# A two-layer mixture-of-experts tower on one core: reciprocal roots by Newton steps on VectorE, one gelu per unit, and four passes written out

## The chip, the cores and the metric

The kernel runs on one core of a Trainium2 chip. The time is the device time of one execution, in microseconds (us). It was taken three times; the median is what is to be forecast. One more execution was recorded by the hardware profiler; all rows below are from it. The engines are TensorE (PE, with its weight loads as PEld), VectorE (DVE), ScalarE (ACT), GpSimd (POOL) and SyncE (SP, which issues the transfers).

## What is computed

Sixteen sequences of 256 tokens go through an embedding and four blocks, each with a residual. The first RWKV block with its channel mix comes first and is not touched. Then come a dense mixture of eight experts, a second RWKV block, and an attention block with a mixture of four experts:

```python
# dense mixture: every expert computes every token (layer 0)
h = gelu(einsum('td,edh->eth', xf, W1) + b1, approximate=False)      # 8 experts, 1024 hidden
out = einsum('etd,te->td', einsum('ehd...', h, W2) + b2, weights)    # weights: softmax over the top 2
# attention (layer 1): 16 heads of 16, q and k normalised per head
_rms = lambda x, w: x * rsqrt(mean(x * x, -1) + EPS) * w
q, k, v = _rms(heads(wq), qn_w), _rms(heads(wk), kn_w), heads(wv)
attn = softmax(causal(q @ k.T * 16 ** -0.5));  x = x + (attn @ v) @ wo.T
# mixture of layer 1: gelu experts o0, o2, o3, and o1 = silu(xf @ e1_w1.T) * (xf @ e1_w2.T) @ e1_down.T
```

The change concerns `gelu`, the `rsqrt` of q and k in `_rms`, and the code of the loop over tokens.

## The kernel before

Matrix products are done in bfloat16 in three parts (high by high, low by high, high by low), so each activation is needed as a rounded half `hi` and a remainder `lo`. Phase A (the embedding and the first RWKV block) fills the first 458 us. After it, `phase_bc` goes over eight tiles of 512 tokens in ten passes. In pass i three streams are woven together: the dense mixture of tile i, the *front* of tile i-1 (RWKV, then attention, two sequences or four 128-token groups `s` to a tile), and the second-layer experts of tile i-2. Pass 0 has the dense mixture alone, pass 1 adds the front, passes 2 to 6 have all three (order `ORDER_BC`), pass 7 has dense units and front (`ORDER_B`), pass 8 front and experts of two tiles (`ORDER_CC`), and pass 9 only experts.

**Order.** Every engine runs the same list of steps. `ORDER_F` is a string of front steps with numbers between them; `plan.braid` puts dense and expert units in where the numbers leave room. `go` walks the list and each engine does its own part of each step. So an engine's queue is fixed, and what stands behind a waiting instruction waits as well.

**Units.** A dense unit `U` (lines 2247 on PE) or a gelu expert unit `I` (line 2000) computes a 128 x 512 product into one of two PSUM banks, `ub[n % 2]` (in rows: `c_up`). ACT reads the bank twice with Gelu: line 1569 writes `g` in float32 (`c_g`), line 1570 writes `hi` in bfloat16 (`c_hi`). POOL then computes `lo` = `g` - `hi` (line 1408). PE may overwrite the bank two units later, when `hi` is written (`bank_free`). The gated expert `G` uses tanh (1560), two DVE operations (1922, 1926) and a copy of `g` to `hi` (1562). The down products (2264, with bias product 2261; experts 2320) add up in PSUM, and DVE takes them into the residual with a weight per token (line 1937, `h`).

**The keys.** For each 128-token group `s`, PE computes q and k (step `Q`), ACT squares and copies them (`Qx`, lines 1485 to 1490), and DVE sums the squares per head (`squares`, 1764), makes the mean (1767) and its reciprocal (1769), and the remainder of v (1771). After two groups, step `X` has ACT take the square root of the reciprocals, 128 x 64 (1497, `c_qrs`). Step `K` on DVE multiplies q and k by it and by the gains and splits them (1779, 1784, 1791 to 1794, 1796, 1798); step `T` has PE transpose them (2090). This happens for groups 0 and 1 (called b0 here) and again for groups 2 and 3 (b1) of each tile. The second group's K and T come after the first's.

**Table loads.** ACT holds one set of functions at a time. Gelu, exp and the square root are in different sets, and a change shows as `ACT_TABLE_LOAD` at the line that needs it.

**The loop.** Passes 0 to 2 and 7 to 9 are written out. Passes 3 to 6 are one hardware loop (`Fori(3, TILES - 1)`) on every engine and on SP's stream of weights.

## Time and profile before

| | before |
|---|---|
| time, median of 3 (range) | 3157.91 us (3155.34 to 3163.25) |
| the profiled execution: time / span | 3164.51 us / 3162.7 us |
| PE busy | 2791.1 us, 88% |
| DVE busy | 1643.0 us, 52% |
| ACT busy | 1819.6 us, 58% |
| POOL busy | 1428.1 us, 45% |

A span is what the trace covers; the time has about 1.8 us around it. Busy time is that in which an engine executes something other than register, branch, semaphore and transfer-issuing instructions. "L" with a number is the line of the kernel.

### The profile page before, as it was taken

To read this page: it belongs to the slowest core of one execution; us is meant where nothing else is said; L and a number is where in the kernel's file an instruction comes from. 1 tells how busy PE (TensorE), PEld (TensorE's weight loads), DVE (VectorE), ACT (ScalarE), POOL (GpSimd) and SP (SyncE) were. 2 spreads that over 40 slices of the span, in tenths; PEclk is the share of its full clock that TensorE was granted. 3 is DMA by queue.
4 is the path that set the end of the run, shared out by engine and by line. 5 is a ranking of instruction groups with operands and counts; after the bars stand their busy time and mean duration, and the time that the engine had idled before them with its cause. 6 is when DMAs were issued, how large, how long until landed. Compare 5 with 4: busy or idle time off the path is not lost. (4 is left out here: it accounts for less than half of the span.)

```text
span 3162.7 us, 58694 instructions
## 1 busy us (share of the span) xinstructions
PE 2791.1 (88%) x22208; PEld 1862.8 (59%) x22208; DVE 1643.0 (52%) x3100; ACT 1819.6 (58%) x2899; POOL 1428.1 (45%) x1358
## 2 busy tenths in 40 slices
PE   3899958998999989998989898989898998987878
PEld 1555535665665666566656675667565765653555
DVE  5776735436446444644365436634563465446452
ACT  3666635555765666565565565565556655654634
POOL 5666523443454435443544454444444443453334
PEclk8999979999999999999999999999999999999999
DMA  1000028621121212121212122212222121210002
GB/s 62 21 27 13 20 74 309 239 102 66 54 92 68 78 68 93 67 82 61 96 68 82 65 81 73 89 64 74 80 82 73 66 74 61 73 41 22 24 23 76
DMA packets 59719, 235.92 MB, mean 75 GB/s; under 512 B 6560, under 2 KB 25024, under 8 KB 40640
## 3 DMA queue, kind: packets, MB, share of 16 engines
q1 hardware_dynamic: 57920, 228.13, 20.6%
q0 software_dynamic: 1536, 4.20, 0.5%
q8 instruction: 176, 2.88, 0.4%
q14 instruction: 87, 0.71, 0.1%
HBM read 200.57 MB, written 31.72 MB: 73 GB/s over the span
## 5 line engine op out<-in xcount | busy, mean ns | idle before, releaser
L1408 POOL TENSOR_TENSOR c_lo<-c_g,c_hi 128x512 bf16<-128x512 f32 x720 | 887.6, 1240 | 1347.0 <-ACT c_hi L1570 1222.3
L2247 PE MATMUL c_up<-c_xT,c_ring 128*128 128x512 bf16 x3072 | 750.8, 384 | 69.3 <-ACT c_hi L1570 56.0
L2264 PE MATMUL c_down<-c_ring,c_hi 128*128 128x256 bf16 x4096 | 715.4, 275 | 0.0
L1569 ACT ACTIVATE c_g<-c_up,b 128x512 f32<-128x512 f32 x512 | 352.9, 689 | 491.1 <-PE c_up L2247 487.1
L2264 PE MATMUL c_down<-c_ring,c_lo 128*128 128x256 bf16 x2048 | 563.3, 275 | 0.0
L2247 PEld LDWEIGHTS c_up<-c_xT,c_ring 128*128 128x128 bf16 x3072 | 295.7, 99 | 367.4 <-ACT c_hi L1570 67.5
L2264 PEld LDWEIGHTS c_down<-c_ring,c_hi 128*128 128x128 bf16 x4096 | 398.3, 99 | 106.0 <-issue 2.2
L1570 ACT ACTIVATE c_hi<-c_up,b 128x512 bf16<-128x512 f32 x512 | 350.9, 685 | 0.0
L1836 DVE CAST c_room<-c_room 128x384 bf16<-128x384 f32 x256 | 128.2, 530 | 403.7 <-PE c_front L2159 307.8
L1569 ACT ACTIVATE c_g<-c_up 128x512 f32<-128x512 f32 x176 | 105.5, 600 | 295.1 <-PE c_up L2000 289.0
L2264 PEld LDWEIGHTS c_down<-c_ring,c_lo 128*128 128x128 bf16 x2048 | 202.1, 99 | 25.0
L1386 POOL TENSOR_TENSOR c_room<-c_room 128x384 bf16<-128x384 f32 x176 | 169.6, 977 | 61.7 <-DVE c_room L1836 61.7
L2000 PE MATMUL c_up<-c_hi,c_ring 128*128 128x512 bf16 x712 | 177.6, 388 | 17.2 <-ACT c_hi L1570 14.3
L2000 PE MATMUL c_up<-c_yhi,c_ring 128*128 128x512 bf16 x504 | 138.4, 400 | 37.1 <-ACT c_hi L1570 26.2
L2320 PE MATMUL c_down<-c_ring,c_hi 128*128 128x192 bf16 x1024 | 144.0, 259 | 25.0 <-DVE h L1937 25.0
L1937 DVE SCALAR_TENSOR_TENSOR h<-c_down,c_gates,h 128x256 f32<-128x256 f32 (+1 forms) x256 | 106.0, 475 | 80.8 <-PE c_down L2264 80.2
L1525 ACT ACTIVATE c_room<-c_front 128x384 f32<-128x384 f32 x256 | 115.7, 489 | 51.5 <-PE c_front L2135 47.4
L1811 DVE TENSOR_REDUCE c_mx<-c_front 128x2 f32<-128x512 f32 (+1 forms) x192 | 117.8, 682 | 47.5 <-PE c_front L2110 41.5
L1569 ACT ACT_TABLE_LOAD x101 | 129.6, 1283 | 11.0 <-PE c_up L2247 9.3
L2131 PE MATMUL c_front<-c_room,c_kz 128*128 128x256 bf16 (+1 forms) x512 | 120.0, 247 | 18.0 <-ACT c_room L1525 18.0
L2320 PE MATMUL c_down<-c_ring,c_lo 128*128 128x192 bf16 x512 | 132.2, 258 | 0.0
L2000 PEld LDWEIGHTS c_up<-c_hi,c_ring 128*128 128x128 bf16 x712 | 68.5, 99 | 90.3 <-issue 18.4
(339 smaller groups left out, 5438.4 us busy)
## 6 DMA issues: line engine op xcount, KB each, us to landing
c_ring<-kept_dense SPq DMA_DIRECT2D x112, 1024.0 KB, 4.8
c_ring<-kept_experts SPq DMA_DIRECT2D x63, 512.0 KB, 3.4
c_room<-in_WB SPq DMA_DIRECT2D x16, 1024.0 KB, 7.0
kept_dense<-c_ring SPq DMA_DIRECT2D x16, 1024.0 KB, 4.8
c_ring<-kept_experts SPq DMA_DIRECT2D x28, 384.0 KB, 3.4
kept_experts<-c_room SPq DMA_DIRECT2D x9, 512.0 KB, 3.8
c_xT<-kept_xT SPq DMA_DIRECT2D x8, 512.0 KB, 5.2
out<-h SPq DMA_DIRECT2D x8, 512.0 KB, 6.6
```

The lines of the kernel that those rows point to most:

```text
L1386: pool.tensor_tensor(pl[:, n % PB, :], pf[:, n % PB, :], ph[:, n % PB, :], ALU.subtract).then_inc(p_lo_pool.sem, 1)
L1408: pool.tensor_tensor(lo14[:, a, :], g[:, h % 4, :], hi14[:, a, :], ALU.subtract).then_inc(lo_ready.sem, 1)
L1525: act.activation(pf[:, n % PB, :], fb[n % 2][:, 0:3 * P], ACT.Exp).then_inc(p_f.sem, 1)
L1569: act.activation(g[:, h % 4, :], ub[n % 2][:, :], ACT.Gelu, bias=bias)
L1570: act.activation(hi14[:, a, :], ub[n % 2][:, :], ACT.Gelu, bias=bias).then_inc(hi_ready.sem, 1)
L1811: dve.tensor_reduce(o, fb[n % 4][:, :].rearrange("p (h k) -> p h k", k=w), AX.X, ALU.max).then_inc(mx_ready.sem, 1)
L1836: dve.tensor_copy(ph[:, n % PB, :], pf[:, n % PB, :]).then_inc(p_hi.sem, 1)
L2000: m = pe.matmul(bank[:, :], w(wp, k, e * P, P), xs[xp][:, k, :], start=(j == 0 and k == 0), stop=(j == 2 and k == kc - 1))
L2131: pe.matmul(bank[:, lo:lo + w], kz[h % 2][:, h // 2, ks_:ks_ + P], qT[:, h // 2, qs_:SEQ], start=True, stop=False, skip_group_check=True)
L2247: last = pe.matmul(ub[n % 2][:, :], r[:, wp, o + q * P:o + (q + 1) * P], xT[:, xp, q, :], start=(m == 0 and q == 0), stop=(m == 2 and q == ...
L2264: m = pe.matmul(bank, (hi14, lo14)[xp][:, a, s * P:(s + 1) * P], r[:, wp, o + KC * P:o + CHUNK], start=False, stop=(k == HC0 - 1 and n == ...
L2320: m = pe.matmul(ob[s // 2][:, (s % 2) * D:(s % 2) * D + DZ], (hi14, lo14)[xp][:, a, s * P:(s + 1) * P], E(plan, wp, name, k, 0, DZ), start ...
```

## The change

Three edits. First, the gelu of a `U` or `I` unit reads the bank once, into `g`; `hi` is a copy of `g`, and PE may overwrite the bank when `g` is written. Second, step `X` and ACT's square root are gone. DVE computes 1 / sqrt(mean) itself, from a shift of the float's bits and three Newton steps, inside `squares` of the odd group; the sum of squares now signals ACT one operation earlier. Third, the loop over passes 3 to 6 is a Python loop, so that the program has these passes written out four times. In the order, the cost `+3.5 X +1.3` becomes `+4.8`, which leaves the units where they were.

```diff
-    return ("Q%d Q%d +1.3 Qx%d Qx%d +3.5 X%d +1.3 K%d +5 T%d Tx%d K%d +4 T%d Tx%d +3"
+    return ("Q%d Q%d +1.3 Qx%d Qx%d +4.8 K%d +5 T%d Tx%d K%d +4 T%d Tx%d +3"
...
-            with eng.Fori(3, TILES - 1) as i:
+            for i in range(3, TILES - 1):
                 go(ORDER_BC, dense(i, PLAN_BC, PLAN_BC), front(i - 1), gates(i - 2))
...
-                def roots(b):
-                    def f():
-                        act.wait_ge(ss_ready.sem, ss_ready.at(t, 2 * b + 2))
-                        act.activation(qrs[:, :, :], inv[:, :, :], ACT.Sqrt).then_inc(q_rstd.sem, 1)
-                    return f
...
-                    act.activation(g[:, h % 4, :], ub[n % 2][:, :], ACT.Gelu, bias=bias)
-                    act.activation(hi14[:, a, :], ub[n % 2][:, :], ACT.Gelu, bias=bias).then_inc(hi_ready.sem, 1)
+                    act.activation(g[:, h % 4, :], ub[n % 2][:, :], ACT.Gelu, bias=bias).then_inc(g_ready.sem, 1)
+                    act.wait_ge(g_ready.sem, g_ready.at(i, plan.gelu[u] + 1))
+                    act.activation(hi14[:, a, :], g[:, h % 4, :], ACT.Copy).then_inc(hi_ready.sem, 1)
...
                         dve.wait_ge(qk_sq.sem, qk_sq.at(t, s + 1))
-                        F.done(dve.tensor_reduce(ss[:, s % 2, :], qsq.rearrange("p (h d) -> p h d", h=2 * HEADS), AX.X,
-                                                 ALU.add))
-                        F.settle()
+                        dve.tensor_reduce(ss[:, s % 2, :], qsq.rearrange("p (h d) -> p h d", h=2 * HEADS), AX.X,
+                                          ALU.add).then_inc(ss_ready.sem, 1)
+                        dve.wait_ge(ss_ready.sem, ss_ready.at(t, s + 1))
                         F.done(dve.tensor_scalar(ms[:, s % 2, :], ss[:, s % 2, :], 1.0 / HD, EPS1, ALU.mult, ALU.add))
-                        F.settle()
-                        dve.reciprocal(inv[:, s % 2, :], ms[:, s % 2, :]).then_inc(ss_ready.sem, 1)
...
+                        if s % 2:
+                            roots()
+                def roots():
+                    root, half = inv[:, :, :], ss[:, :, :]
+                    F.settle()
+                    F.done(dve.tensor_scalar(qrs[:, :, :].bitcast(I32), ms[:, :, :].bitcast(I32), 1, None,
+                                             ALU.logical_shift_right))
+                    F.done(dve.tensor_scalar(half, ms[:, :, :], -0.5, None, ALU.mult))
+                    F.settle()
+                    F.done(dve.tensor_scalar(root.bitcast(I32), qrs[:, :, :].bitcast(I32), -1.0, 1597463007.0, ALU.mult,
+                                             ALU.add))
+                    for n in range(NEWTON):
+                        F.settle()
+                        F.done(dve.tensor_tensor(ms[:, :, :], root, root, ALU.mult))
+                        F.settle()
+                        F.done(dve.tensor_tensor(ms[:, :, :], ms[:, :, :], half, ALU.mult))
+                        F.settle()
+                        if n < NEWTON - 1:
+                            F.done(dve.scalar_tensor_tensor(root, ms[:, :, :], 1.5, root, ALU.add, ALU.mult))
+                        else:
+                            dve.scalar_tensor_tensor(qrs[:, :, :], ms[:, :, :], 1.5, root, ALU.add,
+                                                     ALU.mult).then_inc(q_rstd.sem, 1)
...
-                            pe.wait_ge(hi_ready.sem, hi_ready.at(i, plan.hid[v] + 1))
+                            pe.wait_ge(g_ready.sem, g_ready.at(i, plan.gelu[v] + 1))
```

`F.settle()` makes DVE wait for its own last write.

The next rows are ACT's queue in pass 1, at the squares of groups 2 and 3 (b1): the copies of q, k and v, then dense units. Before:

```order
546 L1485 ACTIVATE c_room<-c_front 128x512 [waits c_k_stack,c_ss_ready,c_qk_ps]
547 L1486 ACTIVATE c_room<-c_front 128x512
548 L1489 ACTIVATE c_room<-c_front 128x256 [waits c_v_lo,c_v_ps]
549 L1490 ACTIVATE c_vh<-c_front 128x16x16
550 L1569 ACTIVATE c_g<-c_up,b 128x512 [waits c_lo_ready,c_up_ps]
551 L1570 ACTIVATE c_hi<-c_up,b 128x512
552 L1497 ACT_TABLE_LOAD
553 L1497 ACTIVATE c_qrs<-c_inv 128x64 [waits c_ss_ready]
554 L1569 ACT_TABLE_LOAD [waits c_lo_ready]
555 L1569 ACTIVATE c_g<-c_up,b 128x512 [waits c_up_ps]
556 L1570 ACTIVATE c_hi<-c_up,b 128x512
```

And with the change:

```order
543 L1488 ACTIVATE c_room<-c_front 128x512 [waits c_k_stack,c_ss_ready,c_qk_ps]
544 L1489 ACTIVATE c_room<-c_front 128x512
545 L1492 ACTIVATE c_room<-c_front 128x256 [waits c_v_lo,c_v_ps]
546 L1493 ACTIVATE c_vh<-c_front 128x16x16
547 L1565 ACTIVATE c_g<-c_up,b 128x512 [waits c_lo_ready,c_up_ps]
548 L1567 ACTIVATE c_hi<-c_g 128x512 [waits c_g_ready]
549 L1565 ACTIVATE c_g<-c_up,b 128x512 [waits c_lo_ready,c_up_ps]
550 L1567 ACTIVATE c_hi<-c_g 128x512 [waits c_g_ready]
```

Two table loads and the square root have left this queue, and every second read of a bank is now a copy that waits for the read before it.

The next rows are DVE's queue in pass 1, from the squares of an odd group to its K. Before:

```order
408 L1764 TENSOR_REDUCE c_ss<-c_room 128x32 [waits c_qk_sq]
409 L1767 TENSOR_SCALAR c_ms<-c_ss 128x32 [waits c_f_steps]
410 L1769 RECIPROCAL c_inv<-c_ms 128x32 [waits c_f_steps]
411 L1771 TENSOR_TENSOR c_vl<-c_room,c_vh 128x256 [waits c_v_hi]
412 L1937 SCALAR_TENSOR_TENSOR h<-c_down,c_gates,h 128x256 [waits c_dn0,c_used_up]
413 L1937 SCALAR_TENSOR_TENSOR h<-c_down,c_gates,h 128x256
414 L1937 SCALAR_TENSOR_TENSOR h<-c_down,c_gates,h 128x256 [waits c_dn1]
415 L1937 SCALAR_TENSOR_TENSOR h<-c_down,c_gates,h 128x256
416 L1779 TENSOR_TENSOR c_room<-c_room,c_qrs 128x512 [waits c_q_rstd]
```

With the change (the three steps of the Newton loop repeat; the middle six rows are left out):

```order
409 L1766 TENSOR_TENSOR c_vl<-c_room,c_vh 128x256 [waits c_v_hi]
410 L1776 TENSOR_SCALAR c_qrs<-c_ms 128x64 [waits c_f_steps]
411 L1778 TENSOR_SCALAR c_ss<-c_ms 128x64
412 L1780 TENSOR_SCALAR c_inv<-c_qrs 128x64 [waits c_f_steps]
...
419 L1784 TENSOR_TENSOR c_ms<-c_inv 128x64 [waits c_f_steps]
420 L1786 TENSOR_TENSOR c_ms<-c_ms,c_ss 128x64 [waits c_f_steps]
421 L1791 SCALAR_TENSOR_TENSOR c_qrs<-c_ms,c_inv 128x64 [waits c_f_steps]
422 L1956 SCALAR_TENSOR_TENSOR h<-c_down,c_gates,h 128x256 [waits c_dn0,c_used_up]
423 L1956 SCALAR_TENSOR_TENSOR h<-c_down,c_gates,h 128x256
424 L1956 SCALAR_TENSOR_TENSOR h<-c_down,c_gates,h 128x256 [waits c_dn1]
425 L1956 SCALAR_TENSOR_TENSOR h<-c_down,c_gates,h 128x256
426 L1798 TENSOR_TENSOR c_room<-c_room,c_qrs 128x512 [waits c_q_rstd]
```

Twelve operations now stand on DVE between the squares and the four updates of `h`, which stood right behind the squares before.

## Rows read from the trace of the kernel before

**Rows 1.** Who waited for whom on PE: total us, times, longest; last row pass 0 alone.

```profile
PE c_up L2247 <- ACT c_hi L1570: 56.0, 36, 4.0
PE c_up L2000 <- ACT c_hi L1570: 40.6, 16, 5.5
...
PE c_up L2247 <- ACT c_hi L1570: 10.8, 6, 4.0
```

**Rows 2.** Timeline, pass 3, b1: ACT, PE and DVE around the square root.

```profile
1467.01 0.63 ACT L1569 ACTIVATE c_g<-c_up 128x512 f32<-128x512 f32 x1
1468.14 1.28 ACT L1497 ACT_TABLE_LOAD   x1
1468.18 1.47 PE L2247 MATMUL c_up<-c_xT,c_ring 128*128 128x512 bf16 x6 [1.50 <-ACT c_hi L1570]
1469.73 0.69 DVE L1779 TENSOR_TENSOR c_room<-c_room,c_qrs 128x512 f32<-128x512 f32 x1 [1.53 <-ACT c_qrs L1497]
1472.33 1.04 PE L2000 MATMUL c_up<-c_yhi,c_ring 128*128 128x512 bf16 x4 [2.68 <-ACT c_hi L1570]
```

**Rows 3.** Stretch behind the 2.68 us wait: length, busy (instructions), PEclk, DMA, GB/s.

```profile
1473.70:1476.50 2.80, 2.80 (x10) 1.15 (x9) 2.46 (x6) 0.60 (x1) 1.31 (x2) 0.50 0.01 3
```

**Rows 4.** Timeline, pass 3, b1, further on: DVE, and PE's step T3.

```profile
1476.54 0.69 DVE L1926 SCALAR_TENSOR_TENSOR c_g<-c_sl,c_up 128x512 f32<-128x512 f32 x1 [0.38 <-PE c_up L2000]
...
1481.45 0.61 PE L2090 MATMUL c_front<-identb,c_qs 128*128 128x128 bf16 x8
```

**Rows 5.** Groups by line, PE: busy, mean ns, idle time before and what ended it.

```profile
L2000 PE MATMUL c_up<-c_yhi,c_ring 128*128 128x512 bf16 x504 | 138.4, 400 | 37.1 <-ACT c_hi L1570 26.2 <-issue 8.2 <-DVE c_g L1926 2.6
```

**Rows 6.** Timeline of PE, entry of passes 3 and 4: start, length, line, [idle before].

```profile
1253.48 1.03 PE L2000 MATMUL c_up<-c_yhi,c_ring 128*128 128x512 bf16 x4
...
1580.55 1.03 PE L2000 MATMUL c_up<-c_yhi,c_ring 128*128 128x512 bf16 x4 [2.97 <-issue]
```

**Rows 7.** Passes 3 and 4 as stretches; columns as in 3.

```profile
1247.00:1570.90 323.90, 301.88 (x2475) 204.00 (x2474) 160.98 (x302) 192.13 (x304) 146.88 (x133) 0.98 0.22 77
1570.90:1895.80 324.90, 299.86 (x2475) 202.12 (x2473) 163.57 (x302) 192.16 (x304) 146.84 (x133) 0.99 0.22 77
```

**Rows 8.** Timeline of PE: a wait of pass 3.

```profile
1264.07 0.61 PE L2000 MATMUL c_up<-c_yhi,c_ring 128*128 128x512 bf16 x2 [2.46 <-ACT c_hi L1570]
```

**Rows 9.** Stretches behind that wait, in pass 3 and in pass 4; columns as in 3.

```profile
1266.00:1269.00 3.00, 3.00 (x8) 1.02 (x7) 2.56 (x9) 1.53 (x4) 1.52 (x2) 0.53 0.00 0
1590.00:1593.00 3.00, 1.85 (x9) 0.90 (x10) 2.93 (x5) 2.34 (x5) 3.00 (x3) 1.00 0.00 0
```

**Rows 10.** Transfers of instructions, pass 2 and then pass 4: packets, MB, share.

```profile
q8 instruction: 20, 0.33, 0.4%
...
q8 instruction: 21, 0.34, 0.4%
```

**Rows 11.** Groups by line, ACT; columns as in 5.

```profile
L1562 ACT ACTIVATE c_hi<-c_g 128x512 bf16<-128x512 f32 x32 | 20.2, 630 | 66.9 <-DVE c_g L1926 66.9
L1497 ACT ACT_TABLE_LOAD x16 | 20.5, 1283 | 0.3
```

**Rows 12.** Timeline of POOL and DVE, pass 3: small operations on DVE beside `lo`.

```profile
1264.10 2.27 POOL L1408 TENSOR_TENSOR c_lo<-c_g,c_hi 128x512 bf16<-128x512 f32 x2 [0.53 <-ACT c_hi L1570]
...
1264.26 1.07 DVE L1966 TENSOR_TENSOR lg<-lg 128x64 f32<-128x64 f32 x1
...
1266.48 0.23 DVE L1969 TENSOR_TENSOR lg<-lg,c_below 128x64 f32<-128x64 f32 x1
1266.74 0.22 DVE L1972 TENSOR_TENSOR lg<-lg 128x64 f32<-128x64 f32 x1
```

**Rows 13.** Timeline of DVE, pass 3, b0: the start of K0.

```profile
1377.01 0.69 DVE L1779 TENSOR_TENSOR c_room<-c_room,c_qrs 128x512 f32<-128x512 f32 x1 [3.81 <-ACT c_qrs L1497]
```

**Rows 14.** Timeline, pass 1, b1: DVE's updates of `h`, and PE's down product.

```profile
838.92 1.65 DVE L1937 SCALAR_TENSOR_TENSOR h<-c_down,c_gates,h 128x256 f32<-128x256 f32 x4
...
840.14 0.27 PE L2261 MATMUL c_down<-b2s,sel 128*128 128x256 bf16 x1
```

More of the change, by code:

```diff
@@ L815, in keys_order @@
     s, r = 2 * b, 2 * b + 1
-    return ("Q%d Q%d +1.3 Qx%d Qx%d +3.5 X%d +1.3 K%d +5 T%d Tx%d K%d +4 T%d Tx%d +3"
-            % (s, r, s, r, b, s, s, s, r, r, r))
+    return ("Q%d Q%d +1.3 Qx%d Qx%d +4.8 K%d +5 T%d Tx%d K%d +4 T%d Tx%d +3"
+            % (s, r, s, r, s, s, s, r, r, r))
 ORDER_F = " ".join((
@@ L897, in __init__ @@
         self.dense, self.experts = dense, experts
-        self.up, self.bank_user, self.hid, self.group, self.gate = {}, [], {}, {}, {}
+        self.up, self.bank_user, self.hid, self.group, self.gate, self.gelu = {}, [], {}, {}, {}, {}
         n_hid = n_group = 0
@@ L903, in __init__ @@
                 self.bank_user.append(u)
+                self.gelu[u] = len(self.gelu)
             elif u[0] == "G":
@@ L1002, in phase_bc @@
 def phase_bc(nc, c, out):
-    KF, KE, KR = 109, 17, TILES * SUB + 5 + 13 + 2 * sum(kind != "B" for kind, _ in FIRST_LOADS)
+    NEWTON = 3
+    KF, KE, KR = 109 - 4 + 2 * (3 + 3 * NEWTON - 1), 17, TILES * SUB + 5 + 13 + 2 * sum(kind != "B" for kind, _ in FIRST_LOADS)
     PB = GROUP
@@ L1132, in phase_bc @@
                               for n in ("hi_ready", "lo_ready"))
+        g_ready = Both(x.enter_context(nc.semaphore("c_g_ready")), NB, len(PLAN_C.gelu))
         half_used = Both(x.enter_context(nc.semaphore("c_half_used")), E0, 0)
@@ L1330, in _ @@
             streamed(2, PLAN_BC, PLAN_B)
-            with sp.Fori(3, TILES - 1) as i:
+            for i in range(3, TILES - 1):
                 streamed(i, PLAN_BC, PLAN_BC)
@@ L1548, in front @@
                         **{"Qx%d" % s: qkv(s) for s in range(SUB)}, **{"Tx%d" % s: stacks(s) for s in range(SUB)},
-                        **{"X%d" % b: roots(b) for b in range(SEQS)},
                         **{"Nx%d" % b: negated(b) for b in range(SEQS)}, **{"O%d" % b: output(b) for b in range(SEQS)},
@@ L2220, in bank_free @@
                         else:
-                            pe.wait_ge(hi_ready.sem, hi_ready.at(i, plan.hid[v] + 1))
+                            pe.wait_ge(g_ready.sem, g_ready.at(i, plan.gelu[v] + 1))
                     elif before is not None and before.dense:
-                        pe.wait_ge(hi_ready.sem, hi_ready.at(i, n - 1))
+                        pe.wait_ge(g_ready.sem, g_ready.at(i, n - 1))
                     elif before is not None:
```

## The prediction

> **What bounds the kernel now.** I read the page first: PE is busy 88% of the span, every other engine under 60%. So the end moves only with what PE waits for, and I read PE's waits before anything else. The list of waits has ACT's second gelu read at its head, 36 waits of 56.0 us and 16 of 40.6 us [rows 1]: PE wants a PSUM bank and ACT is late. The timeline says why. In b1 of a steady pass (2 to 6) PE stands 1.50 us and then 2.68 us, and between the two ACT loads the square root's table, 1.28 us, computes the root, and loads gelu's back [rows 2]. Behind them TensorE has its lower clock: the granted share is 0.50, 1.2 GHz instead of 2.4 [rows 3]. A second limit lies close by on DVE: K2, the four updates of `h`, the gated product and K3 follow each other with 0.38 us of idle time, and PE's T3 at 1481.45 starts as K3 ends [rows 4]. So PE's waits for ACT at b1 are not all on the path. If they go, PE comes to T2 and T3 earlier and waits for DVE there.
>
> **The loop written out.** PE waits 8.2 us in all at these matmuls for nothing that the profile shows ("issue") [rows 5]. They are the loop's turns: pass 3 is entered without a wait, pass 4 after 2.97 us [rows 6]. Written out, three such waits go, -8.2 us. But pass 3, which has no turn in front, is only 1.0 us shorter than pass 4 (323.90 against 324.90), with 2.0 us more of PE busy time [rows 7]. Pass 3 has a wait of 2.46 us for ACT a little later [rows 8], and so has pass 4. Behind it the clock is 0.53 in pass 3, and 1.00 in pass 4, which had stood at the turn shortly before [rows 9]. Eight matmuls take pass 3 3.00 us, nine take pass 4 1.85: 8 x (0.375 - 0.206) = 1.3 us that pass 3 pays [rows 9]. I give this back in three passes: -8.2 + 3.9 = **-4.3 us**. Bounds: 3 x 1.0 = -3.0 by the lengths [rows 7], -8.2 by the waits. The longer program fetches no more: a written-out pass brings 0.33 MB of instructions and a looped one 0.34 MB [rows 10].
>
> **Gelu read once.** In b1, `g` runs from 1467.01 to 1467.64, and PE starts at 1468.18, when `hi` is done [rows 2]. With the change PE is let go at the end of `g`, 0.54 us earlier. `hi` itself comes later. The copy of a float32 tile takes 0.63 us [rows 11], as long as the gelu it replaces, but can't overlap the operation that it waits for. From start to start the old pair is 1.13 us, the new one 0.63 + 0.63 and a little, so ACT loses some 0.15 us per unit, and POOL's `lo` and the down products get their input that much later. There are PE waits for all this to help, 52 [rows 1], so its bound is 52 x 0.54 = -28 us. I count them by place. Pass 0 has six, 10.8 us [rows 1], four of them long: -2.2. In a steady pass one at the start of the front [rows 8] and two in the heads of b0: 3 x 0.54 = -1.6. The other ones come before DVE's RWKV chain, which PE waits for anyway, or are the pair of b1, counted below. Against it stands +0.7 a pass for exps and output copies that queue on ACT behind copies (a handful of places by 0.15). Five passes: -4.5. Passes 8 and 9 have a few: -1.0. Sum **-7.7 us**. Bounds: 0, if the lateness of `hi` eats it all, and -28.
>
> **Roots on DVE.** Removed: 16 square roots and 32 table loads, 16 of them on 1497 for 20.5 us [rows 11] and as many back to gelu, together 41 us of ACT. ACT is no bound, so this counts only at the places where PE waits for it. Added: twelve operations of 128 x 64 on DVE, nearly each waiting for the one before, less one reciprocal per group. A two-source operation of this size takes 0.22 us and its follower starts 0.26 us later [rows 12]. That makes 12 x 0.25 = 3.0 us from the end of the v remainder to K, less 0.2 for the reciprocal. No row shows such an operation on the bits as integers; I take the float rows, since shape and type width are the same.
> There is a higher price. While POOL works on `lo` the same operations take 1.07 us, not 0.22 [rows 12], each until POOL is done. So one POOL operation in the Newton steps costs up to 0.85 us, and three of them 2.6.
> At b0 of a steady pass K0 starts 3.81 us after DVE's last operation, since gelu stood ahead of the root in ACT's queue [rows 13]. Newton steps make it 2.8 with POOL idle: T0, for which PE waits, gains **-0.9**, five times -4.5. With two POOL operations it is +0.7.
> At b1 K2 starts 1.53 us after DVE's last operation [rows 2], and with Newton 2.8 after it: +1.3. The 1.50 and 2.68 us waits and the slow clock behind them go from PE (some 5.5 us), but T3 follows DVE's chain [rows 4], so what counts is that chain. It gets +1.3 for Newton, -0.4 for the idle time that the gated product no longer has, up to -1.7 where two of K's own operations no longer meet POOL, and up to +2.6 for three POOL operations that now run beside it, since ACT without loads feeds POOL sooner. I take **+1.0** of -1.0 to +3.5: nearer to the contended rows, since `lo` operations stand close there. Five times: +5.0.
> In passes 1 and 7 there is also the queue: four updates of `h` (1.65 us) run at once behind the squares while ACT takes the root, and PE's next down product needs the first two at 840.14 [rows 14]. Newton's 2.8 us go ahead of them, which makes the first two end at 838.9 + 2.8 + 0.8 = 842.5, and PE wait some 2 us; with K later, +2.5 per pass, +5.0. Pass 8: +1.1. Sum of the roots **+6.6 us**, bounds -12 and +22.
>
> **Two rules weighed.** The rows say that a small DVE operation waits out a POOL operation [rows 12]. The Trainium skill, page "SBUF — State Buffer", section "SBUF: two separate sides", says that a DVE operation with two SBUF inputs and a GpSimd operation that reads SBUF exclude each other for a whole instruction. Nine of the twelve have two such inputs, so the page speaks against this edit, and the trace agrees in kind (1.07 against 0.22 us). The rows give 1.28 us for a load, and the next operation on ACT starts at its end, since load, root and K follow from 1468.14 to 1469.73 [rows 2]. The Trainium skill, page "ScalarE: Activation LUTs", section "What ACT_TABLE_LOAD costs", adds a drain and gives 2.66 us for a switch. By it the 32 would be 85 us of ACT in place of 41; no row here has the drain, and the sum stays.
>
> **The sum.** -4.3 - 7.7 + 6.6 = -5.4 us. The profiled execution took 3164.5 us, 6.6 over the median of the three runs, so it becomes 3159.1; set against the median, 3157.9 - 5.4 = **3152.5 us**. About 0.3%, 9.5 us, is what a measurement can tell from no change.
>
> **Rivals.**
> *DVE's chain has room (faster).* If POOL and the Newton steps miss each other, b1 gives -1.0 in place of +1.0 (-10 us), passes 1 and 7 lose 1 us each less (-2), and the shortened 2.46 us wait no longer brings the slow clock in (-1.3 in five passes, -6.5). Together -18.5: 3134 us. For it: PE loses some 5.5 us per pass there now. Against it: T3 sits right behind K3 [rows 4].
> *DVE becomes the bound (slower).* POOL's `lo` meets the Newton steps everywhere: b1 +3.5 (+12.5 over the forecast), b0 +0.7 (+8): 3173 us. It decides from three `lo` operations in each b1, if b0 has one as well: then some +15 over the sum, +9.5 in all. For it: 1.07 us [rows 12]. Against it: one `lo` needs a unit, and PE makes no unit while it waits.
> *The loop's turn gives nothing.* Writing it out moves the wait to a fetch elsewhere, or the slow clock takes all of it, as passes 3 and 4 nearly say [rows 7]: 3157 us.
>
> **How the numbers follow.** Forecast 0.48 (faster 0.16, same 0.30, slower 0.02); DVE with room 0.22, faster; DVE the bound 0.20 (slower 0.18, same 0.02); loop's turn gives nothing 0.10 (same 0.06, slower 0.04). Together faster 0.38, same 0.38, slower 0.24. The forecast's own range is 3144 to 3161. The range for all reaches most of the way to both outer cases, 3136 to 3169, and leaves out one in ten at either end.
>
> **What the profile after would show.** Right: 32 table loads fewer; no "issue" wait of over 2 us at the entry of passes 4 to 6, and in its place a clock near 0.5 some 15 us later; PE's bank waits end at the end of `g`; in b1 the 1.50 and 2.68 us waits gone or under 1 us, and PE waiting at T2 or T3 for DVE's last K operation; DVE's small operations at 0.22 to 0.26 us apart, some of them 1.1 us; in passes 1 and 7 a PE wait of about 2 us at 2261 for `h`. The prediction fails if T2 and T3 bring no wait (then it was too high), if most of the Newton operations take over 1 us, or if the slow clock comes at other places than now: a stretch of it costs about 1.3 us.

## The result: 0.4% slower

The changed kernel took 3170.32 us (median of 6 runs, 3165.32 to 3172.92) against 3157.55 us before (6 runs, 3154.6 to 3163.25). The ratio is 1.0036, 95% interval 1.0024 to 1.0049. The forecast was 3152.5 us, in a range of 3136 to 3169, so the sign was wrong and the time lies outside.

I read PE's waits of the changed kernel first; they answer to [rows 1]. The next rows are the list of waits: total us, times, longest.

```profile
PE c_front L2109 <- DVE c_qs L1815: 42.5, 14, 5.6
...
PE c_up L2266 <- ACT c_g L1565: 31.7, 30, 3.7
...
PE c_up L2019 <- ACT c_g L1565: 22.2, 9, 5.5
...
PE c_down L2280 <- DVE h L1956: 15.9, 6, 3.7
```

The waits for a free bank fell from 96.6 to 53.9 us. But PE now waits 42.5 us for the transposed keys of DVE (11.8 us before) and 15.9 us for `h` at 2280 (6.9 before; 11.0 and 6.9 of these stand in pass 0, which has no roots).

The next rows are the stretches of the changed kernel, cut where SP issues the next tile's load: passes 1 to 3, and passes 7 to 9 together. Columns as in [rows 3].

```profile
655.90:927.90 272.00, 239.94 (x2004) 166.94 (x2002) 137.22 (x273) 157.76 (x238) 110.13 (x105) 0.95 0.19 69
927.90:1255.60 327.70, 303.83 (x2482) 208.16 (x2483) 172.57 (x326) 192.17 (x298) 147.57 (x135) 0.97 0.22 75
1255.60:1576.50 320.90, 299.81 (x2474) 205.19 (x2472) 169.62 (x322) 192.04 (x297) 146.14 (x133) 0.98 0.23 77
...
2539.10:3171.00 631.90, 530.61 (x4268) 349.04 (x4266) 314.02 (x661) 333.85 (x519) 247.08 (x231) 0.93 0.15 49
```

Cut in the same way for before and for four of the experiments below, in us. Each column is one profiled execution. Those of before and of `roots_only` are not typical: 6.6 us above and 7.0 us below the median of their kernels. And a single pass can move by more than its edit: pass 0 is the same program in before, `loop_only` and `roots_only`, and took 200.2, 195.9 and 198.7.

| pass | before | changed | loop_only | gelu_only | roots_only | gelu_and_loop |
|---|---|---|---|---|---|---|
| 0 | 200.2 | 198.7 | 195.9 | 198.0 | 198.7 | 198.7 |
| 1 | 262.9 | 272.0 | 263.5 | 265.0 | 270.9 | 264.1 |
| 2 | 325.8 | 327.7 | 325.4 | 325.7 | 327.8 | 325.5 |
| 3 | 323.9 | 320.9 | 320.4 | 323.4 | 323.2 | 320.7 |
| 4 | 324.9 | 320.9 | 318.1 | 324.5 | 327.6 | 320.8 |
| 5 | 324.6 | 320.9 | 321.1 | 324.4 | 327.8 | 319.1 |
| 6 | 324.1 | 320.8 | 320.2 | 324.3 | 327.5 | 319.1 |
| 7 to 9 | 618.2 | 631.9 | 615.3 | 617.2 | 627.2 | 611.7 |

So the changed kernel gains 14 us in passes 3 to 6 and loses 9 us in pass 1, 2 in pass 2 and 14 in passes 7 to 9. The large losses are in the passes that have a front but not all three streams.

Pass 1 shows the loss at its simplest. The next rows are the changed kernel's timeline of DVE, PE and POOL at the first K of pass 1.

```profile
765.01 0.23 DVE L1786 TENSOR_TENSOR c_ms<-c_ms,c_ss 128x64 f32<-128x64 f32 x1
765.27 1.06 DVE L1791 SCALAR_TENSOR_TENSOR c_qrs<-c_ms,c_inv 128x64 f32<-128x64 f32 x1
766.26 1.65 DVE L1956 SCALAR_TENSOR_TENSOR h<-c_down,c_gates,h 128x256 f32<-128x256 f32 x4
767.83 1.55 DVE L1798 TENSOR_TENSOR c_room<-c_room,c_qrs 128x512 f32<-128x512 f32 x1
769.41 1.59 DVE L1803 TENSOR_TENSOR c_room<-c_room,qkw 128x256 f32<-128x256 f32 x2
...
767.34 0.27 PE L2280 MATMUL c_down<-b2s,sel 128*128 128x256 bf16 x1
...
765.07 1.19 POOL L1411 TENSOR_TENSOR c_lo<-c_g,c_hi 128x512 bf16<-128x512 f32 x1 [6.09 <-ACT c_hi L1567]
767.67 2.72 POOL L1411 TENSOR_TENSOR c_lo<-c_g,c_hi 128x512 bf16<-128x512 f32 x2 [1.42 <-ACT c_hi L1567]
```

And the same place before:

```profile
767.22 0.69 DVE L1779 TENSOR_TENSOR c_room<-c_room,c_qrs 128x512 f32<-128x512 f32 x1 [0.47 <-ACT c_qrs L1497]
767.95 0.76 DVE L1784 TENSOR_TENSOR c_room<-c_room,qkw 128x256 f32<-128x256 f32 x2
...
768.05 0.27 PE L2261 MATMUL c_down<-b2s,sel 128*128 128x256 bf16 x1
...
765.70 1.16 POOL L1408 TENSOR_TENSOR c_lo<-c_g,c_hi 128x512 bf16<-128x512 f32 x1 [6.09 <-ACT c_hi L1570]
769.84 2.57 POOL L1408 TENSOR_TENSOR c_lo<-c_g,c_hi 128x512 bf16<-128x512 f32 x2 [2.99 <-ACT c_hi L1570]
```

The Newton steps are as cheap as forecast (0.26 us from start to start; only the last one meets POOL). K starts at 767.83, where it was 767.22. PE's down product ahead of the keys starts 0.7 us sooner (767.34, before 768.05), so for PE K comes 1.3 us later. And before, ACT's two table loads kept gelu back, and so POOL: K's first three operations were done (1.5 us) before `lo` came at 769.84. Now `lo` comes at 767.67, and the same three take 3.2 us. PE waits 3.20 us for the keys, where it waited 0.19 and 0.68: 1.3 us for the later start and 1.7 for the slower operations. Behind that wait it has its lower clock, which it didn't have there before; the next rows are PE's transposes and the stretch behind them (columns as in [rows 3]).

```profile
772.45 0.62 PE L2109 MATMUL c_front<-identb,c_qs 128*128 128x128 bf16 x8 [3.20 <-DVE c_qs L1815]
...
773.00:776.00 3.00, 3.00 (x22) 2.33 (x20) 2.75 (x9) 2.88 (x3) 0.00 (x0) 0.50 0.00 0
```

In b1 of a steady pass the two bank waits are gone or small, as forecast, and PE waits 4.59 us for the keys instead. There POOL meets the Newton steps themselves. The next rows are the timeline of DVE and POOL in pass 3.

```profile
1473.57 1.06 DVE L1786 TENSOR_TENSOR c_ms<-c_ms,c_ss 128x64 f32<-128x64 f32 x1
1474.66 1.17 DVE L1789 SCALAR_TENSOR_TENSOR c_inv<-c_ms,c_inv 128x64 f32<-128x64 f32 x1
1475.86 1.20 DVE L1784 TENSOR_TENSOR c_ms<-c_inv 128x64 f32<-128x64 f32 x1
...
1473.35 3.63 POOL L1411 TENSOR_TENSOR c_lo<-c_g,c_hi 128x512 bf16<-128x512 f32 x3 [3.40 <-ACT c_hi L1567]
...
1481.34 0.93 PE L2109 MATMUL c_front<-identb,c_qs 128*128 128x128 bf16 x7 [4.59 <-DVE c_qs L1815]
```

Three `lo` operations, three small operations of 1.1 to 1.2 us: the contended case of the forecast, 2.7 us more.

In b0 of a steady pass the steps miss POOL, and K meets it; in b1 of pass 8 `lo` operations stand beside five of the steps, of 1.06 to 1.20 us each (one is shown). The next rows are the gain operations of K0 in pass 3 (0.76 us before) with POOL beside them, then pass 8.

```profile
1383.02 2.56 DVE L1803 TENSOR_TENSOR c_room<-c_room,qkw 128x256 f32<-128x256 f32 x2
...
1382.65 2.65 POOL L1411 TENSOR_TENSOR c_lo<-c_g,c_hi 128x512 bf16<-128x512 f32 x2 [6.06 <-ACT c_hi L1567]
...
3000.53 1.20 DVE L1789 SCALAR_TENSOR_TENSOR c_inv<-c_ms,c_inv 128x64 f32<-128x64 f32 x1
...
2997.90 6.33 POOL L1411 TENSOR_TENSOR c_lo<-c_g,c_hi 128x512 bf16<-128x512 f32 x5 [9.51 <-ACT c_hi L1567]
...
3007.28 0.50 PE L2109 MATMUL c_front<-identb,c_qs 128*128 128x128 bf16 x3 [5.58 <-DVE c_qs L1815]
```

### The profile page after: what moved, and what is told of

It reads as the page before. It is cut to its first block and busy times, and to the rows that moved or that the text cites. A ratio compares the mean times of both kernels' runs of the same rounds, so it can differ in the third digit from the quotient of the medians.

```text
span 3171.0 us, 56103 instructions
## 1 busy us (share of the span) xinstructions
PE 2797.4 (88%) x22208; PEld 1883.7 (59%) x22208; DVE 1693.2 (53%) x3260; ACT 1820.8 (57%) x2851; POOL 1420.7 (45%) x1358
## 5 line engine op out<-in xcount | busy, mean ns | idle before, releaser
L1411 POOL TENSOR_TENSOR c_lo<-c_g,c_hi 128x512 bf16<-128x512 f32 x720 | 879.9, 1227 | 1384.7 <-ACT c_hi L1567 1231.6
L2283 PEld LDWEIGHTS c_down<-c_ring,c_hi 128*128 128x128 bf16 x4096 | 400.1, 99 | 106.3 <-issue 1.3
L1567 ACT ACTIVATE c_hi<-c_g 128x512 bf16<-128x512 f32 x688 | 433.3, 630 | 22.0
L2339 PE MATMUL c_down<-c_ring,c_hi 128*128 128x192 bf16 x1024 | 153.4, 268 | 27.8 <-DVE h L1956 27.8
L1956 DVE SCALAR_TENSOR_TENSOR h<-c_down,c_gates,h 128x256 f32<-128x256 f32 x256 | 106.0, 474 | 85.4 <-PE c_down L2283 85.4
L2019 PE MATMUL c_up<-c_yhi,c_ring 128*128 128x512 bf16 x504 | 131.9, 385 | 13.7 <-ACT c_g L1565 11.0
L2339 PEld LDWEIGHTS c_down<-c_ring,c_hi 128*128 128x128 bf16 x1024 | 102.4, 108 | 35.1 <-issue 30.5
```

The lines of the kernel that those rows point to most:

```text
L1411: pool.tensor_tensor(lo14[:, a, :], g[:, h % 4, :], hi14[:, a, :], ALU.subtract).then_inc(lo_ready.sem, 1)
L1567: act.activation(hi14[:, a, :], g[:, h % 4, :], ACT.Copy).then_inc(hi_ready.sem, 1)
L2019: m = pe.matmul(bank[:, :], w(wp, k, e * P, P), xs[xp][:, k, :], start=(j == 0 and k == 0), stop=(j == 2 and k == kc - 1))
L2283: m = pe.matmul(bank, (hi14, lo14)[xp][:, a, s * P:(s + 1) * P], r[:, wp, o + KC * P:o + CHUNK], start=False, stop=(k == HC0 - 1 and n == ...
L2339: m = pe.matmul(ob[s // 2][:, (s % 2) * D:(s % 2) * D + DZ], (hi14, lo14)[xp][:, a, s * P:(s + 1) * P], E(plan, wp, name, k, 0, DZ), start ...
```

## The experiments

Each run is compared with the kernel before on the same chip; the ratio is given with its 95% interval.

### Each edit alone

`loop_only` is the kernel before with this edit alone, for the engines and for SP:

```diff
-            with eng.Fori(3, TILES - 1) as i:
+            for i in range(3, TILES - 1):
```

> The kernel before, with only the loop over passes 3 to 6 written out. All theories: 2 to 5 us faster (three turns of 2.4 to 3.0 us go, and the lower clock behind the 2.46 us wait comes back in those passes, 1.3 us each). If writing out were the cause of the loss, it would be 5 us or more slower, with issue waits spread over PE.

Measured: 3138.58 us, 0.9923 (0.9908 to 0.9939), 24 us faster. Every theory was too low.

`gelu_only` is the kernel before with the read of the bank, the copy and PE's wait on `g`:

```diff
-                    act.activation(hi14[:, a, :], ub[n % 2][:, :], ACT.Gelu, bias=bias).then_inc(hi_ready.sem, 1)
+                    act.wait_ge(g_ready.sem, g_ready.at(i, plan.gelu[u] + 1))
+                    act.activation(hi14[:, a, :], g[:, h % 4, :], ACT.Copy).then_inc(hi_ready.sem, 1)
```

> The kernel before, with only the gelu read once. Theory 1 (the roots on DVE cause the whole loss): 4 to 8 us faster. Theory 2 (the copy that waits for its gelu makes hi, lo and ACT's copies of the keys late, and that is the loss of passes 1, 7 and 8): 5 us or more slower, and in pass 1 the wait of PE at the first scores is near 2.1 us as in the changed kernel, not 1.3.

Measured: 3161.59 us, 0.9997 (0.9986 to 1.0007). Neither theory: no gain, no loss. The next rows are its list of waits of PE.

```profile
PE c_up L2003 <- ACT c_g L1571: 38.4, 15, 5.5
PE c_up L2250 <- ACT c_g L1571: 38.1, 36, 3.7
PE c_down L2323 <- DVE h L1940: 27.9, 7, 5.4
PE c_front L2025 <- ACT c_xhi L1477: 20.7, 8, 4.3
```

The bank waits fell by 20 us, from the 96.6 of [rows 1], so the edit does what it says. But PE waits 8.7 us more for `xhi` (20.7; it was 12.0), 2.9 us more for `h` at the experts' down product (25.0 before), and the rest in smaller waits. The `xhi` wait grows by 1.3 to 1.6 us in each of passes 2 to 6. ACT isn't late there: it stands idle 2.29 us before `xhi` and waits for DVE's RWKV chain (it was 0.81). The chain itself is 1.0 us longer in passes 3 to 6, since one more of its operations now meets a `lo`. The next rows are pass 4 before, and then with the edit.

```profile
1661.25 0.68 DVE L1723 TENSOR_TENSOR c_room<-c_room 128x512 f32<-128x512 f32 x1
1667.64 0.63 ACT L1475 ACTIVATE c_xhi<-c_room 128x512 bf16<-128x512 f32 x1 [0.81 <-DVE c_room L1734]
```

```profile
1655.23 1.68 DVE L1726 TENSOR_TENSOR c_room<-c_room 128x512 f32<-128x512 f32 x1
1655.21 1.15 POOL L1410 TENSOR_TENSOR c_lo<-c_g,c_hi 128x512 bf16<-128x512 f32 x1 [0.45 <-ACT c_hi L1573]
1662.62 0.63 ACT L1477 ACTIVATE c_xhi<-c_room 128x512 bf16<-128x512 f32 x1 [2.29 <-DVE c_room L1737]
```

Passes 2 to 6 together are 1.0 us shorter. Pass 0 is 2.2 us shorter, but it differs by up to 4.3 us between kernels that share its program, so this shows no gain.

`roots_only` is the kernel before with step X and ACT's `roots` taken out and DVE's `roots()` put into `squares`, as in the change.

> The kernel before, with only the roots by Newton steps on DVE. Theory 1 (the roots on DVE cause the whole loss): 18 to 26 us slower in passes 1, 7 and 8 and some 2 us faster in all of passes 2 to 6, so 16 to 24 us slower; in pass 1 a wait of about 3 us of PE for the first transposed keys, of about 2.4 us for h, and a longer time at the lower clock behind them. Theory 2 (the copy is the cause): within 5 us of before. Theory 3 (only both together): 0 to 8 us slower.

Measured: 3195.38 us, 1.0103 (1.0085 to 1.0121), 32 us slower. That is above all three theories. Theory 1 has the place right (pass 1 +8, passes 7 to 9 +9), but the steady passes lose too: passes 4 to 6 are each 3 us longer, where I expected a small gain.

`gelu_and_loop` is the changed kernel without the roots edit.

> The changed kernel with the roots back on ScalarE (gelu read once and passes written out stay). Theory 1: 8 to 13 us faster than before, the sum of the two edits alone. Theory 2: as slow as before or slower. It would be the version that beats both.

Measured: 3138.77 us, 0.9932 (0.9914 to 0.995). It beats both kernels, and it is no better than the written-out loop alone. The three edits alone sum to -24 - 1 + 32 = +7 us; together they gave +11. Each of these numbers is uncertain by 3 to 6 us, so there is no interaction to be seen in the whole.

Against `gelu_and_loop` the changed kernel differs by the roots alone, and both have the passes written out. The two profiled executions are 33.7 us apart: 7.9 in pass 1, 6.0 in passes 2 to 6 and 20.1 in passes 7 to 9. And PE's busy time, for the same 22208 matmuls, is 23.5 us of it (2797.4 against 2773.9), at a granted clock of 0.955 against 0.966. So PE's waits grew by only some 10 us; the larger part I read as PE working at its lower clock behind them. Not all of it need be the roots': 6.6 us of the 20.1 stand behind the last transposes of keys in pass 8, 159.5 us against 152.9, and there the kernel before, which has no Newton steps, took 159.8.

### What the roots cost

`one_newton_step` and `two_newton_steps` (they make the roots less exact):

```diff
-    NEWTON = 3
+    NEWTON = 1
```

> The changed kernel with one Newton step instead of three (six operations fewer on VectorE at each of 16 places, some 1.5 us each; the roots are less exact). Theory N (the length of the Newton steps is what costs): PE's waits for the first transposed keys shrink by 1.5 us each, total 15 to 25 us faster than the changed kernel, so a ratio to before of 0.995 to 0.999. Theory P (POOL's lo meets the operations of K, because ACT no longer pauses for the table loads): less than half of that, as K's own operations still take 1.2 to 1.6 us beside POOL: ratio 0.999 to 1.003.

> The changed kernel with two Newton steps. From three steps to one the time fell by 34 us. If every step costs the same (the chain from the squares to the transposed keys is what PE waits for throughout): halfway, ratio 0.998. If the cost comes at a threshold, where the steps push K's operations into POOL's lo: near one of the two ends, 0.993 to 0.995 or 1.001 to 1.004.

Measured: one step 3131.94 us, 0.9928 (0.9914 to 0.9943); two steps 3142.03 us, 0.9953 (0.9941 to 0.9965). From the changed kernel's 1.0036 the third step costs 26 us and the second 8. Six operations of 0.26 us at 16 places are 25 us of DVE; 34 went. So the length matters, and by more than either theory said, but it is not the same for each step: the third costs more than its 12 us on DVE.

`table_pause_back` keeps the Newton steps and gives ACT its two table loads back, with a square root of a constant that nobody reads:

```diff
+                        act.wait_ge(ss_ready.sem, ss_ready.at(t, 2 * b + 2))
+                        act.activation(c.scr[:, 2:3], c.b1[:, 0:1], ACT.Sqrt, scale=0.0)
```

> The changed kernel, with the Newton steps on VectorE, and besides them one square root of a constant on ScalarE at the old place, for nothing but its two table loads (32 more in all, 41 us of ACT). Theory P (the loads used to hold back gelu and with it POOL, so that K's operations had the shared time to themselves): K's operations at T0 of passes 1 and 7 go from 1.3 to 1.5 us to 0.4 to 0.7, and the kernel is no slower than the changed one, perhaps 5 us faster. Theory N (only the length of the Newton steps counts): 5 to 15 us slower, as ACT's waits come back in b1 of every pass on top.

Measured: 3156.86 us, 1.0004 (0.9993 to 1.0014). To add 32 table loads, 41 us of useless work, to ACT made the changed kernel 10 us *faster*. The next rows are its timeline of DVE and POOL at the first K of pass 1.

```profile
763.86 0.67 DVE L1805 TENSOR_TENSOR c_room<-c_room,c_qrs 128x512 f32<-128x512 f32 x1
764.56 0.76 DVE L1810 TENSOR_TENSOR c_room<-c_room,qkw 128x256 f32<-128x256 f32 x2
765.36 1.20 DVE L1817 CAST c_qs<-c_room 128x256 bf16<-128x256 f32 x1
...
765.25 2.51 POOL L1411 TENSOR_TENSOR c_lo<-c_g,c_hi 128x512 bf16<-128x512 f32 x2 [2.97 <-ACT c_hi L1574]
```

K's first operations are back at 0.67 and 0.76 us. But the casts meet POOL instead, PE's wait at this place stays at 3.4 us, and pass 1 is no shorter (273.0 against 272.0). PE's waits for the keys fell from 42.5 to 21.5 us in all, most of it in passes 2 to 6, where 4.59 us became 1.42. Yet passes 3 to 6 took 1283.4 us in all, against 1283.5: the waits for a bank came back instead (71.1 us, from 53.9). The gain is in pass 2 (3.8 us) and in passes 7 to 9 (11.0 us), and there it is mostly the clock: PE's busy time is 9.5 us shorter. The next rows are passes 7 to 9 of `gelu_and_loop` and of `table_pause_back` (columns as in [rows 3]), to be read against the last row of the changed kernel above, 530.61 and 0.93.

```profile
2525.60:3137.30 611.70, 518.72 (x4268) 342.22 (x4265) 304.84 (x621) 344.59 (x531) 247.99 (x231) 0.96 0.15 50
```

```profile
2533.60:3154.50 620.90, 521.14 (x4268) 342.87 (x4265) 314.78 (x661) 344.51 (x531) 247.03 (x231) 0.95 0.14 50
```

So this run shows that a pause of ACT can pay, but not that it pays by leaving K alone.

`lo_zero_newton` and `lo_zero_sqrt` are the changed kernel and `gelu_and_loop`, with POOL kept from reading:

```diff
-                        pool.tensor_tensor(lo14[:, a, :], g[:, h % 4, :], hi14[:, a, :],
-                                           ALU.subtract).then_inc(lo_ready.sem, 1)
+                        pool.memset(lo14[:, a, :], 0.0).then_inc(lo_ready.sem, 1)
```

> The changed kernel, with lo of the dense and expert units left out: POOL writes zeros there and reads nothing, so that nothing of VectorE waits for these operations (the output lacks the low parts). To be read against the next one. Theory P (POOL beside VectorE is a good part of what the roots cost): the roots on VectorE cost here under 15 us, against some 33 with lo computed; all small operations are near 0.23 us. Theory N (the steps' own length): still 25 us or more.

> The same with the roots on ScalarE by square root (gelu read once, passes written out, lo left out). The difference of the two gives the cost of the roots on VectorE with POOL out of the way: theory P under 15 us, theory N 25 us or more. Both should be faster than with lo computed, as PE's down products no longer wait for POOL.

Measured: with Newton steps 3018.36 us, 0.9559 (0.9547 to 0.9571); with the square root 3035.25 us, 0.9608 (0.9595 to 0.9621). With `lo` out of the way the Newton steps are 17 us *faster* than the square root; with `lo` they are 32 us slower. So the steps themselves are worth having here, and it takes POOL's `lo` to turn them into a loss. The next rows are the groups of DVE by line, of `lo_zero_newton` and then of the changed kernel.

```profile
L1785 DVE TENSOR_TENSOR c_ms<-c_ms,c_ss 128x64 f32<-128x64 f32 x48 | 10.8, 225 | 1.6
L1788 DVE SCALAR_TENSOR_TENSOR c_inv<-c_ms,c_inv 128x64 f32<-128x64 f32 x32 | 7.2, 225 | 1.1
```

```profile
L1786 DVE TENSOR_TENSOR c_ms<-c_ms,c_ss 128x64 f32<-128x64 f32 x48 | 18.5, 385 | 1.6
L1789 DVE SCALAR_TENSOR_TENSOR c_inv<-c_ms,c_inv 128x64 f32<-128x64 f32 x32 | 13.8, 433 | 1.1
```

The pair also shortens POOL (529 ns for a zero tile against 1227) and so every `lo` wait of PE. That part is in both runs; that it drops out of their difference is argued, not shown, so of the 49 us between -17 and +32 the share of the slowed operations on DVE is open.

The slowed operations can be read from the traces. The next table has the time from the end of the odd group's squares to the end of the DVE operation that PE's first transpose of the keys waits for (1815 in the changed kernel), in us:

| place | gelu_and_loop | changed | table_pause_back | lo_zero_newton |
|---|---|---|---|---|
| b0 of passes 1 and 7 | 6.7 | 10.2 | 10.4 | 8.1 |
| b1 of passes 1 and 7 | 6.8 | 8.5 | 9.4 | 7.7 |
| b0 of passes 2 to 6 | 7.5 | 8.0 | 7.1 | 6.6 |
| b1 of passes 2 to 6 | 5.5 | 9.0 | 8.9 | 6.2 |
| b0 of pass 8 | 6.6 | 8.9 | 7.2 | 6.6 |
| b1 of pass 8 | 6.6 | 10.8 | 10.9 | 6.6 |

Without `lo` the steps shorten this chain or leave it where it was, except in passes 1 and 7 and at b1 of a steady pass. With `lo` they lengthen it at every place. `table_pause_back` shortens it by more than 0.1 us only at b0 of the steady passes and of pass 8.

`pe_filled` gives PE something to do in the longest waits:

```diff
+                        if s == (0 if t in (0, TILES - 2, TILES - 1) else 2):
+                            pe.wait_ge(v_hi.sem, v_hi.at(t, 2 * (s // 2 + 1)))
+                            spare = stack_banks(s)[0][:, :].bitcast(BF16)
+                            for _ in range(24):
+                                pe.transpose(spare[:, 0:P], c.identb[:, :], c.identb[:, :])
```

> The changed kernel, with 24 transposes of a constant on PE (2.6 us at the higher clock) ahead of the first or third transposed keys, where PE waits 3.2 to 5.6 us now; they go to a free bank and are overwritten. Theory C (the lower clock behind these waits is a good part of the loss): the granted clock stays at 1.00 behind T0 or T2, and it is 5 to 12 us faster than the changed kernel. If the clock has little part: within 3 us of it, or slower by what the transposes add where the wait is shorter.

Measured: 3163.54 us, 1.0021 (1.0011 to 1.0031), some 5 us faster than the changed kernel. The two stretches at the lower clock behind T0 of pass 1 are gone from its trace. So the clock is a part of the loss. The 5 us are what this edit gives back, and not all that the clock costs: it fills one wait of each front. PE still waits 5.57 us at T2 of pass 8, with the lower clock behind it, and PE's busy time without the roots was 23.5 us shorter, as read above.

`newton_behind_h` makes the steps a step X of DVE, at the old place, so that the updates of `h` go first:

```diff
-                        if s % 2:
-                            roots()
...
+                        **{"X%d" % b: roots for b in range(SEQS)},
```

> The changed kernel with the Newton steps as a step of their own at the old place X, behind the updates of h where these stood between the squares and X. If the updates of h queued behind Newton cost time: PE's wait of 2.4 us for h in b1 of passes 1 and 7 is gone, 4 to 6 us faster than the changed kernel, ratio 1.002. If K's lateness takes it all back, the same as the changed kernel, 1.0036.

Measured: 3171.78 us, 1.0049 (1.0035 to 1.0063): the same as the changed kernel or a little slower. In pass 1 the wait of 2.37 us for `h` is gone, and PE waits 3.58 us for the keys a little later instead.

`split_roots` does all three steps for each group by itself:

```diff
-                        if s % 2:
-                            roots()
+                        if s % 2 == 0:
+                            roots(0)
...
                 def stack(s):
                     def f():
+                        if s % 2:
+                            roots(1)
```

> The changed kernel with all three Newton steps, but done for each group by itself on 128 x 32: for the even group right behind its squares, where VectorE waits some 0.9 us for ScalarE anyway, and for the odd group behind the even group's K. VectorE has 12 operations more per pair in all. If what counts is how late K of the even group starts: T0 waits 1 to 2 us less in passes 1, 7 and 8, ratio to before 0.996 to 1.001. If VectorE's whole chain through T3 counts (both groups), it is no faster than the changed kernel, 1.003 or more, as the odd group's steps add 2.6 us between the two K.

Measured: 3179.81 us, 1.0068 (1.0055 to 1.008), slower than the changed kernel. In pass 1 the first wait for keys fell to 1.69 us, but the odd group's became 2.95. The chain through the second K counts.

### What the loop cost

`four_loops` and `two_loops` are the kernel before with passes 3 to 6 as four loops of one turn, or two of two:

```diff
-            with eng.Fori(3, TILES - 1) as i:
-                go(ORDER_BC, dense(i, PLAN_BC, PLAN_BC), front(i - 1), gates(i - 2))
+            for first in (3, 5):
+                with eng.Fori(first, first + 2) as i:
+                    go(ORDER_BC, dense(i, PLAN_BC, PLAN_BC), front(i - 1), gates(i - 2))
```

> The kernel before, with passes 3 to 6 as four hardware loops of one turn each. No loop turns back, but the waits in them still use a register's value, as in the kernel before. If the turns are what the loop cost: as fast as written out, ratio 0.992 to 0.996. If the waits on computed values inside are: 0.998 or more.

> The kernel before, with passes 3 to 6 as two hardware loops of two turns each: two turns back in place of three, and all four passes still inside a loop whose waits use a register's value. If the turns alone cost the 24 us: a third of it goes, 8 us, ratio 0.9975. If the cost lies mostly in every pass inside a real loop (waits of two semaphores or more, each with its value worked out, 0.9 us from start to start in the gated product against 0.7 written out): 0 to 3 us, ratio 0.999 or more, pass 3 near 324 us and passes 3 and 5 (entered without a turn) 1 us shorter than 4 and 6.

Measured: four loops 3135.99 us, 0.9926 (0.991 to 0.9941), as fast as written out; two loops 3166.92 us, 1.0028 (1.0017 to 1.0039), not faster than one loop of four turns though it has a turn less. My premise for four loops was wrong. Their profile has 56051 instructions and the written-out kernel's 55991, against 58694 before and 58375 with two loops: with a single turn nearly all of the instructions that a loop adds inside its passes are gone as well. So four loops don't part the turns from the waits. Two loops do: a turn less gained nothing. What is left is what passes 3 to 6 have in common in a loop that really turns. The trace shows a piece of it: the two operations of a gated product, before in pass 3,

```profile
1485.71 0.69 DVE L1922 SCALAR_TENSOR_TENSOR c_sl<-c_sl,c_up 128x512 f32<-128x512 f32 x1 [3.01 <-ACT c_sl L1560]
1486.62 0.69 DVE L1926 SCALAR_TENSOR_TENSOR c_g<-c_sl,c_up 128x512 f32<-128x512 f32 x1 [0.22 <-DVE c_sl L1922]
```

and in `loop_only`:

```profile
1478.51 0.69 DVE L1922 SCALAR_TENSOR_TENSOR c_sl<-c_sl,c_up 128x512 f32<-128x512 f32 x1 [2.68 <-ACT c_sl L1560]
1479.23 0.69 DVE L1926 SCALAR_TENSOR_TENSOR c_g<-c_sl,c_up 128x512 f32<-128x512 f32 x1
```

Between them stand several waits whose values depend on the pass: 0.91 us from start to start in the loop, 0.72 written out. In `four_loops` it is 0.72 as well (but for one meeting another work), in `two_loops` 0.90. On ACT, where back-to-back operations have no such waits between them, the distances are the same to a nanosecond. I read this as the time that an engine needs to work out the value of each wait, which is only argued from these places; that all 24 us come from it isn't shown. Of the 25.9 us between the profiled executions of before and `loop_only`, 17.6 lie in passes 3 to 6, in many small pieces; how many of them are such waits stays open. The other 8 lie where the two programs are the same, and that of before was 6.6 us slower than its median.

### The fastest

`one_step_no_gelu_edit` has the loop written out and the roots by one Newton step, and reads gelu twice.

> Passes written out and the roots by one Newton step, but gelu read twice from its bank as before. The gelu edit alone gave nothing. If it gives nothing here too, this is as fast as the run with one step and the gelu edit, 0.991 to 0.994. If its waits for the copy meet the roots: 0.990 or less, the best version.

Measured: 3130.16 us, 0.9918 (0.9905 to 0.9931). It can't be told from one step with the gelu edit (0.9928), nor from `loop_only` (0.9923). So of all three edits only the written-out loop is shown to pay.

## Why the prediction was wrong

**The loop, forecast -4.3, measured -24.** The step that failed is "pass 3, which has no turn in front, is only 1.0 us shorter than pass 4". I took pass 3 for a pass without the loop's costs. It is inside the loop, and written out, pass 3 itself became 3.5 us shorter. What the loop costs in each of its passes was in no term of the sum. The turns' waits were read rightly as idle time, but a turn less (`two_loops`) gained nothing. The lower clock near the entry stands in pass 3 of `loop_only`, as before, and came back in passes 5 and 6, as forecast; in its pass 4 it did not.

**Gelu once, forecast -7.7, measured -1 (-4 to +2).** PE was let go when `g` ends, and the waits for a bank fell by 20 us. The step that failed is the steady passes: -1.6 a pass with only "+0.7 a pass for exps and output copies" against it, 4.5 us in five passes, where passes 2 to 6 gained 1.0 in all. I had called the RWKV chain a chain "which PE waits for anyway", and counted nothing for the bank waits ahead of it, but took its length for fixed. It became 1.0 us longer in passes 3 to 6 of `gelu_only`, as the new times of `lo` put one more POOL operation beside it (1.68 us in place of 0.68), and PE waits for it at `xhi`. The -2.2 of pass 0 is also the difference of the two traces, but no run can tell it from chance.

**Roots on DVE, forecast +6.6, measured +32.** The step that failed is the price of passes 1, 7 and 8, "+2.5 per pass, +5.0. Pass 8: +1.1": the traces with and without the roots put 28 of their 34 us in passes 1 and 7 to 9 (6.6 of them behind the last keys). The wait of some 2 us for `h` came as forecast (2.37 and 2.60). But it was all that I had counted beside a later K. At b0 POOL met K's operations, with a wait of 3.20 us in both passes; in pass 8 it met K at b0 and five of the steps at b1, with waits of 4.92 and 5.58 us (4.01 and 1.71 before). And the lower clock behind these waits, which I had named as a sign of being wrong, was in no term: 16 of the 28 us are busy time of PE.

In the steady passes both terms were off too. At b0 I forecast -0.9: K0 did start 2.80 us behind the v remainder in place of 3.81, but its two gain operations took 2.56 us in place of 0.76, and the keys came 0.5 us later and not 0.9 earlier. At b1 I took +1.0 of -1.0 to +3.5: three `lo` operations met the steps, and the chain became 3.5 us longer. Even so these five passes lost 6 us together (forecast +0.5), since PE's waits for a bank went (76.4 us in `gelu_and_loop`, 53.9 in the changed kernel). Right were the 3 us of the steps alone, the 1.1 us of each beside POOL, and that PE waits for K at b1 in place of the banks. The upper bound of +22 was too low by my own figures: with +3.5 and +0.7 in five passes, +5.0 and +1.1 it is +27.

I also counted the table loads as a cost on ACT alone. In pass 1 they held POOL back until K's first operations were done, as the rows show; what that was worth is open, since the loads put back didn't make pass 1 shorter.

That the whole missed by only 18 us is luck: the loop gave 20 us more than forecast, and the roots cost 26 us more and gelu gave 7 less.

**The rivals.** "DVE becomes the bound", 0.20, is nearest to what happened to this edit: its "three `lo` operations in each b1" were there. But it puts the loss in the steady passes, where little of it was, and its 3173 us, close to the 3170 measured, rests on the wrong price for the loop. The rule of the Trainium skill, page "SBUF — State Buffer", section "SBUF: two separate sides", that a two-input DVE operation and a GpSimd operation that reads SBUF exclude each other, was right against the edit: two-input operations of the steps took 0.225 us on average with POOL only writing, and 0.39 and 0.43 in the rows above with POOL reading. The drain that the Trainium skill, page "ScalarE: Activation LUTs", section "What ACT_TABLE_LOAD costs", adds to a load is in no row here.

## What to carry to other kernels

An engine that pauses may be what keeps a shared resource free for another: before you remove a stall, look which engine it holds back, and what that one will then run beside. A new wait of PE costs more than its length where the lower clock follows it: read the busy time of PE and its granted clock beside the list of waits. Price small operations on DVE by the row beside a POOL operation, not by the free one, wherever POOL is fed by the same event. Read a run by passes as well: a wait that goes at one place can come back at another. And compare a looped pass with a written-out one, not with the pass at the loop's entry, to see what a loop costs.

## What I had not expected of the hardware

Thirty-two table loads added for nothing made a kernel 10 us faster (1.0036 to 1.0004). Casts of one input wait for POOL as well: 1.20 us in place of 0.29 beside a `lo` operation. Passes in a loop that turns cost 3.5 to 6.8 us more of 325 than the same code written out (the table above), while loops of a single turn cost nothing (0.9926 against 0.9923).
